# Output projection and expert routing of a mixture-of-experts layer: two stages, or one stage by batches

## The reference, cut to what matters

```python
hidden = resid + (ctx @ o_w + o_b)
xt = layer_norm(hidden, ln2_w, ln2_b).reshape(T, D)
logits = xt @ router_w
probs = softmax(logits)
top1 = argmax(probs)
top2 = argmax(where(m1 > 0, -inf, logits))
loc1 = cumsum(m1, axis=0) - 1
loc2 = cumsum(m2, axis=0) - 1 + m1.sum(axis=0)
m1 = m1 * (loc1 < C)
m2 = m2 * (loc2 < C)
g1, g2 = (probs * m1).sum(-1), (probs * m2).sum(-1)
xin = einsum('tec,td->ecd', d1 + d2, xt)
```

## Time and profile before

| | us |
|---|---|
| median of 3 runs | 2369.15 (2369.07 to 2370.01) |
| profiled execution, its own time | 2373.17 |
| its span, first to last instruction | 2371.40 |
| DVE busy | 1503.7 (63% of the span) |
| POOL busy | 815.1 (34%) |
| PE busy | 1682.7 (71%) |
| ACT busy | 904.1 (38%) |

### The profile page before, as it was taken

The page is one execution under the profiler, slowest core; times in us unless marked ns, Lnnn a source line. Parts: engine busy times, 40 slices in busy tenths (PEclk is TensorE's granted clock), DMA queues, the critical chain, the costliest instruction groups (busy, mean ns, idle before and its releaser), DMA issues. The chain is left out here.

```text
span 2371.4 us, 37567 instructions
## 1 busy us (share of the span) xinstructions
PE 1682.7 (71%) x12976; PEld 1004.5 (42%) x12976; DVE 1503.7 (63%) x3125; ACT 904.1 (38%) x1669; POOL 815.1 (34%) x911
## 2 busy tenths in 40 slices
PE   4899999996207943599991076589999999610992
PEld 2333333335106732399991044333333333500772
DVE  7888888953502236677774584888889884450223
ACT  4377777773002310000000033437777776200330
POOL 3022222224473420278780670102222222445341
PEclk8599999996558976699996589669999999655996
DMA  4433443300014442000004000443333330001444
GB/s 124 108 73 93 100 111 61 64 2 0 22 49 127 137 127 73 0 1 0 0 0 44 18 10 36 139 78 64 57 62 62 56 56 2 0 29 54 134 137 126
DMA packets 124466, 144.60 MB, mean 61 GB/s; under 512 B 34336, under 2 KB 74656, under 8 KB 123296
## 3 DMA queue, kind: packets, MB, share of 16 engines
q1 hardware_dynamic: 105648, 121.14, 22.1%
q0 software_dynamic: 8192, 16.86, 2.1%
q10 hardware_dynamic: 10480, 4.73, 0.8%
HBM read 96.17 MB, written 45.71 MB: 60 GB/s over the span
## 5 line engine op out<-in xcount | busy, mean ns | idle before, releaser
L723 DVE TENSOR_REDUCE mx<-pA 128x1 f32<-128x512 f32 (+3 forms) x1216 | 723.5, 656 | 46.5 <-PE pA L588 25.1
L748 ACT ACTIVATE wt<-pB 128x512 f32<-128x512 f32 (+1 forms) x1216 | 606.2, 583 | 254.2 <-PE pB L631 254.1
L588 PE MATMUL pA<-ka,qa 48*128 48x512 bf16 (+3 forms) x1536 | 413.2, 344 | 30.9 <-PEq L285 16.6
L631 PE MATMUL pB<-qa,ka 51*128 51x512 bf16 (+3 forms) x1536 | 389.6, 334 | 32.4 <-ACT wt L748 27.5
L788 POOL TENSOR_SCALAR_AFFINE_SELECT wt<-wt 128x512 f32<-128x512 f32 x256 | 162.4, 634 | 676.5 <-ACT wt L748 676.5
L650 PE MATMUL pC<-wt,va 128*32 128x512 f32 (+3 forms) x3072 | 332.5, 506 | 1.3 <-POOL wt L788 1.3
L588 PEld LDWEIGHTS pA<-ka,qa 48*128 48x128 bf16 x1536 | 138.6, 95 | 252.7 <-DVE mx L723 179.4
L1176 POOL DMA_INDIRECT y<-eo,dest x128 | 122.5, 957 | 185.0 <-issue 112.5
L592 PE MATMUL pA<-future_lo,pick_lo 64*128 64x64 bf16 x1024 | 184.3, 196 | 0.0
L592 PE MATMUL pA<-future_hi,pick_hi 64*128 64x64 bf16 x1024 | 181.0, 191 | 0.0
L631 PEld LDWEIGHTS pB<-qa,ka 51*128 51x128 bf16 x1536 | 119.5, 94 | 127.6 <-ACT wt L748 114.9
(11 more groups left out here) (249 smaller groups left out, 2533.8 us busy)
## 6 DMA issues: line engine op xcount, KB each, us to landing
qa<-qk_parts SPq DMA_DIRECT2D x384, 64.0 KB
ka<-qk_parts SPq DMA_DIRECT2D x384, 64.0 KB
w<-in_L_ffn_fc_w_dram SPq DMA_DIRECT2D x64, 256.0 KB, 2.8
xi<-xin SPq DMA_DIRECT2D x32, 258.0 KB, 3.7
qk_parts<-qp SPq DMA_DIRECT2D x24, 256.0 KB, 2.6
qk_parts<-kp SPq DMA_DIRECT2D x24, 256.0 KB, 3.4
xin<-zero SPq DMA_DIRECT2D x4, 1032.0 KB, 9.6
qa<-mT SPq DMA_DIRECT2D x256, 3.0 KB
```

What stands on the lines that cost most here:

```text
L588: last = pe.matmul(out[:, k, :], qa[u % 3][0:KROWS, t * per + k, i * P:(i + 1) * P], ka[u % 3][0:KROWS, t * per + k, a:b], start=True, sto ...
L631: last = pe.matmul(pB[n % NB][:, k * (e - a):(k + 1) * (e - a)], ka[u % 3][rows, h, j * P:(j + 1) * P], qa[u % 3][rows, h, a:e], start=Tru ...
L723: vec.reduce_max(mx[a // HALF][:, i, t * per:(t + 1) * per], pA[n % NA][:, 0:per * (b - a)].rearrange("p (h k) -> p h k", h=per), AX).then ...
L748: act.activation(wt[g % NW][:, heads, 0:e - a], pB[n % NB][:, 0:per * (e - a)].rearrange("p (h q) -> p h q", h=per), ACT.Exp).then_inc(exp ...
```

## The change

`ffn_route` goes away as a block. Its instructions become part of `ffn_output`, batch by batch, so the routing's tiles have 8 x 16 = 128 columns, and there are four times as many instructions on them. `ffn_output` is written out without loops. The places go on from batch to batch: the sums of a batch are carried over into the first tile of the next. First choices of batch b - 1 are routed and their rows scattered after the moments of batch b; second choices are found and counted with them but sent after the last batch, and the gates follow at the end. Where the counts, the places or the kept choices have to live longer than a batch, they have their own memory; `kept` is now copied from the one-hot choice, and the place is made by adding the running sum and subtracting the tile's own. ACT's order interleaves the exponential of a batch with the square root of the next; PE's has the counts of batch b - 1 behind the projection of batch b + 1. POOL's has the scaling of later batches between the scatters of earlier ones.

The diff, cut to its core (in the new `ffn_output`; `two` is `range(2)`, `tiles[b]` and `col[b]` are the slices of batch b):

```diff
-    c["restart"] = core.sb(ctx, "restart", [P, E, TILES])
+    c["restart"] = core.sb(ctx, "restart", [P, E, BT])
...
+                def scatter(n, b):
+
+                    pool.wait_ge(xn_kept, 2 * b + 2)
+                    pool.wait_ge(send_ready, n * BATCH + b + 1)
+                    for t in range(b * BT, (b + 1) * BT):
+                        pool.indirect_dma_start(
+                            out=w["xin"], out_offset=bass.IndirectOffsetOnAxis(ap=keep["send"][:, n, t:t + 1], axis=0),
+                            in_=xt[:, t, :], in_offset=None).then_inc(sent, 16)
+
+                bias(0)
+                bias(1)
+                numbers(0)
+                scaled(0)
+                bias(2)
+                scaled(1)
+                bias(3)
+                pool.wait_ge(c["wiped"], 16 * WIPES)
+                for b in range(BATCH):
+                    scatter(0, b)
+                    if b + 2 < BATCH:
+                        scaled(b + 2)
+                pool.wait_ge(sent, 16 * TILES)
+                numbers(1)
+                for b in range(BATCH):
+                    scatter(1, b)
+                pool.wait_ge(sent, 16 * 2 * TILES)
...
-                staggered(pe, project, logits)
+                def counts(b):
+
+                    pe.wait_ge(one_ready, 2 * b + 2)
+                    for n in two:
+                        flat = one[n][:, :, :].rearrange("p t e -> p (t e)")
+                        pe.matmul(pCount[:, n, 0, :], c["upper"][:, :], flat, start=True, stop=True)
+                        last = pe.matmul(pCount[:, n, 1, :], c["ones"][:, :], flat, start=True, stop=True)
+                    last.then_inc(counted, 1)
+
+                project(0)
+                project(1)
+                logits(0)
+                for b in range(1, BATCH):
+                    if b + 1 < BATCH:
+                        project(b + 1)
+                    counts(b - 1)
+                    logits(b)
+                counts(BATCH - 1)
...
+                side_by_side(1)
+                root(0)
+                transposed(1)
+                logits(0)
+                for b in range(1, BATCH):
+                    if b + 1 < BATCH:
+                        side_by_side(b + 1)
+                    weights(b - 1)
+                    root(b)
+                    if b + 1 < BATCH:
+                        transposed(b + 1)
+                    logits(b)
+                weights(BATCH - 1)
...
+                def choices(b):
+
+                    p = prob[:, tiles[b], :]
+                    vec.wait_ge(exps_ready, b + 1)
+                    link(vec.reduce_sum(total[:, :], p, AX))
+                    link(vec.reciprocal(recip[:, :], total[:, :]))
+                    link(vec.tensor_tensor(p, p, over_e(recip[:, :]), ALU.mult))
+                    top(p, 0, b)
+                    link(vec.scalar_tensor_tensor(logit2[:, :, :], one[0][:, :, :], LOWEST, L[:, tiles[b], :],
+                                                  ALU.mult, ALU.add))
+                    top(logit2[:, :, :], 1, b)
+
+                def located(n, b):
+
+                    place_in = loc[n][:, tiles[b], :]
+                    link(vec.tensor_copy(tot[n][:, :, :], pCount[:, n, 1, :].rearrange("p (t e) -> p e t", e=E)))
+                    if b > 0:
+                        link(vec.tensor_tensor(tot[n][:, :, 0], tot[n][:, :, 0], run[n][b - 1][:, :, BT - 1], ALU.add))
+                    link(vec.tensor_tensor_scan(run[n][b][:, :, :].rearrange("p e t -> p (e t)"),
...
+                    link(vec.scalar_tensor_tensor(place_in, pCount[:, n, 0, :].rearrange("p (t e) -> p t e", e=E), -1.0,
+                                                  run[n][b][:, :, :].rearrange("p e t -> p t e"), ALU.add, ALU.add))
+                    link(vec.tensor_tensor(place_in, place_in, pCount[:, n, 1, :].rearrange("p (t e) -> p t e", e=E),
+                                           ALU.subtract))
+                    link(vec.tensor_copy(kept[n][:, tiles[b], :], one[n][:, :, :]))
+
+                def sends(n, b):
...
+                    vec.tensor_copy(keep["send"][:, n, tiles[b]], place[:, :]).then_inc(send_ready, 1)
+                    vec.wait_ge(send_ready, n * BATCH + b + 1)
+
+                moments(0)
+                normal(0)
+                for b in range(1, BATCH + 1):
+                    if b < BATCH:
+                        moments(b)
+                    largest(b - 1)
+                    choices(b - 1)
+                    if b < BATCH:
+                        normal(b)
+                    vec.wait_ge(counted, b)
+                    located(0, b - 1)
+                    sends(0, b - 1)
+                    located(1, b - 1)
+                for b in range(BATCH):
+                    sends(1, b)
...
-        ffn_route(core, keep, w, c, tag)
```

More of the change, by code:

```diff
@@ L803, in ffn_output @@
         sem = lambda n: core.sem(ctx, n + tag)
+        two = range(2)
         rows, cT = sb("ctx_rows", [P, BCOL]), sb("ctxT", [P, SEQ])
@@ L808, in ffn_output @@
         pT, pO, pX, pL = ps("pT_o", [P, SEQ]), ps("pO", [P, BCOL]), ps("pX_o", [P, SEQ]), ps("pL", [P, BT * E])
+        pCount = ps("pCount", [P, 2, 2, BT * E])
         (rows_ready, bias_added, cT_done, cT_ready, o_done, o_used, var_ready, std_ready, xn_ready, xn_kept, xT_done,
-         xT_ready, l_done, l_kept, dve, pool_chain) = (sem(n) for n in (
+         xT_ready, l_done, l_kept, dve) = (sem(n) for n in (
              "rows_ready", "bias_added", "octx_T_done", "octx_T_ready", "o_done", "o_used", "var_o", "std_rdy_o",
[L812 to L822, removed]
+             "xn_ready_o", "xn_kept", "oxn_T_done", "oxn_T_ready", "l_done", "l_kept", "dve_o"))
+        G, B = [P, TILES, E], [P, BT, E]
+        prob, kept, loc = sb("prob", G), [sb(f"kept{n}", G) for n in two], [sb(f"loc{n}", G) for n in two]
+        shifted, logit2, work, one = sb("shifted", B), sb("logit2", B), sb("work_r", B), [sb(f"top{n}", B) for n in two]
+        tot = [sb(f"tot{n}", [P, E, BT]) for n in two]
+        run = [[sb(f"run{n}_{b}", [P, E, BT]) for b in range(BATCH)] for n in two]
+        best, first, total, recip = (sb(n, [P, BT]) for n in ("best", "first", "total", "recip"))
+        gate, weighed, gates = sb("gate", [P, 2, TILES]), sb("weighed", G), sb("gate_sum", [P, TILES])
+        at, dropped, place = sb("at", [P, BT]), sb("dropped", [P, BT]), sb("place", [P, BT])
+        used, inside = sb("used", [P, E]), sb("inside", [P, E, CC])
+        max_found, exps_ready, one_ready, counted = (sem("max_found"), sem("exps_ready"), sem("one_ready"), sem("counted"))
+        send_ready, sent, number_set = sem("send_ready"), sem("sent"), sem("number_set")
+        over_e = lambda v: v.unsqueeze(2).to_broadcast([P, v.shape[1], E])
+        over_t = lambda v, nt=BT: v.unsqueeze(1).to_broadcast([P, nt, E])
+        col = [slice(b * BCOL, (b + 1) * BCOL) for b in range(BATCH)]
+        tiles = [slice(b * BT, (b + 1) * BT) for b in range(BATCH)]
+        L = keep["logits"][:, :].rearrange("p (t e) -> p t e", e=E)
         with nc.Block() as block:
@@ L897, in batch, with weights, moments @@
                     act.wait_ge(l_done, b + 1)
-                    act.copy(keep["logits"][:, bass.ds(b * BT * E, BT * E)], pL[:, :]).then_inc(l_kept, 1)
+                    act.copy(L[:, tiles[b], :], pL[:, :].rearrange("p (t e) -> p t e", e=E)).then_inc(l_kept, 1)
+                def weights(b):
+                    act.wait_ge(max_found, b + 1)
+                    act.activation(prob[:, tiles[b], :], shifted[:, :, :], ACT.Exp).then_inc(exps_ready, 1)
                 side_by_side(0)
                 transposed(0)
[L902 to L905, removed]
+                side_by_side(1)
[11 more added lines that the diff above has]
+                weights(BATCH - 1)
             @block.vector
             def _(vec):
[L909 to L913, removed]
+                link = Chain(vec, dve).link
+                def moments(b):
+                    hidden = keep["hid"][:, col[b]]
                     vec.wait_ge(bias_added, b + 1)
@@ L926, in batch @@
                     reached(vec, xT_done, b)
[L927 to L964, removed]
@@ L980, in _ @@
[L980 to L988 removed]
+                    vec.wait_ge(one_ready, 2 * b + n + 1)
```

122 lines of the change are left out of this document (45 added, 77 removed).

## The result

The changed kernel takes **2333.15 us** (median of 4 runs, 2331.61 to 2337.55) where the kernel before takes 2369.21 beside it: ratio 0.985, 95% interval 0.9833 to 0.9867, a gain of 36 us. It is faster, as forecast, and inside the range, but the gain is nearly twice the 19 us of the forecast. The profiled execution took 2332.93 us (span 2331.1).

What follows compares the result with a forecast made beforehand. POOL's 64 scatters bound the stage, so their start counts. 101.0 us to the last send plus 61.9 gives 162.9 a layer, winning 10.1 and 9, together 19: 2369.15 - 19 = 2350 us, range 2326 to 2364.

Steps and rivals of the forecast that it cites:

- The mechanism: Routing stage: scatters start per batch, at 42.8 us instead of 81.2; POOL idles between groups, DVE's rounds of some 22 us pace.
- the straight line: DVE routing instructions: price interpolated between 4 and 512 columns, giving 0.292 us at 128 columns.
- the blocks beside POOL's scaling: Routing rounds: DVE instructions with two SBUF operands wait for POOL's running instruction to end; 11.6 us a layer.
- The no-blocking rival: Routing beside POOL's scaling: DVE and POOL run side by side, the 11.6 us a layer fall away; 2327 us, chance 0.18.
- nothing more is given back: Denies the rival for routing: blocks at upper bound, casts waiting for scatters, dearer instructions; 2357 to 2366 us, chance 0.15.
- the instructions shrink: Denies the rival that DVE's 128-column routing instructions keep the 512-column price; 2451 us, chance 0.08.
- Two of the signs: Stage timeline: first scatter 40 to 46 us after the start, last group at about 102.
- the path to the last send: Routing stage, from its start to the last batch's send of first choices: 101.0 us.
- From the last send to the experts: End of the stage: first scatter, spacings at 1.41, second series and final 8.10 us; sum 61.9 us.
- The two rules weighed: Routing: table load taken as 1.28 us, not about 2.66; scatter spacing beside DVE as 1.41, not 1.26.
- The second rival: ACT's table loads: each change of function costs two loads, 7.7 us in all; 2358 us, chance 0.07.

Runs made afterwards that it cites:

- the control: The changed kernel run once more with no edit; 2332.48 us.
- second_late: Changed kernel without POOL's scaling, counts ahead of the next projection, second choices of all batches found after the last first send; 2295.36 us.

## Why the prediction was right, and where its size was off

**The mechanism** holds, but for one term: the prediction let instructions with one SBUF operand run free, and a copy of that kind was stopped too (last section). 3.2 of the 9.2 us stand at this copy; that the two-operand instruction behind it would have waited in its place is likely, but no run shows it. The first scatters start half a stage earlier, POOL idles between groups, and DVE's rounds are the pace, though they took 20.4, 20.7 and 14.4 us rather than some 22. The 128-column instructions cost 0.292 us as the straight line said, and the blocks beside POOL's scaling are there and cost what they last. The no-blocking rival gave 2327 us, nearer to the measured time than 2350, and is wrong all the same: the blocks were seen, lengthened and taken away, each time with the matching change. Of the other rivals: the Exp begins 0.01 us after its table load has ended, so a change of function costs one load of 1.28 us; the casts (L1060) average 188 ns, so nothing more is given back there; and the instructions shrink.

**The size.** The measured 2333 us lies below the forecast's own range of 2340 to 2358; it is inside the whole range only because that reaches down to the no-blocking case. Two of the signs came early as well: the first scatter at 39.9 us, where 40 to 46 were named, and the last group at 95.4 instead of about 102. In the first layer the stage was forecast at 162.9 us and took 155.0. The step that failed is the path to the last send, 101.0 forecast and 94.6 measured:
- The blocks, 11.6 forecast, were 9.2. In batch 1 DVE arrived 1.4 us into POOL's first scaling instruction, so less of it was left to wait for; in batches 1 and 2 a scan got through between the two, and those that read PSUM ran on beside them.
- TensorE's parts came sooner. The logits of batch 0 were kept 20.2 us into the stage instead of 21.8; the eight transposes took 1.09 us, where those of before took 1.97 at a granted clock of 0.55 in the stretch from 541 to 551 us, nearly the lower of its two levels (1.2 of 2.4 GHz), against 0.73 now (rows below). The wait for the counts was 0.85 us instead of 1.6. The two middle rounds, blocks aside, were 0.6 to 0.8 us shorter each. Together 3.6 to 4 us, and not all of it the change's: in the control the same transposes took 1.38 us at 0.66, and the fourth group came 1.0 us later.
- From the last send to the experts 60.3 us instead of 61.9: the spacing of the last group beside DVE was 1.27 us, not 1.41.

The first 10 us of the stage in the kernel before, then in the changed one (busy time by stretch, columns as above; the clock is the third number from the end):

```profile
541.00:551.00 10.00, 6.64 (x31) 6.00 (x32) 0.67 (x3) 4.47 (x5) 4.65 (x2) 0.55 0.00 0
541.00:551.00 10.00, 6.41 (x34) 5.94 (x35) 1.32 (x3) 4.70 (x5) 4.80 (x3) 0.73 0.00 0
```

The second layer was credited with 9 us, of which 1.2 were for a quicker TensorE that was to stay; its stage came out as long as the first's and won 15.7. The two stages together won 33.7 us in these traces, 31.7 in the control's, against 19. That leaves 2 to 4 us of the measured 36 outside the stages, within the 9 us by which that part differs from trace to trace; I take it for no effect of the change.

**The two rules weighed.** The table load: the trace after decides for the row, 1.28 us, against the 2.66 us with a drain that the Trainium skill (ScalarE: Activation LUTs, What ACT_TABLE_LOAD costs) gives; no drain shows between load and Exp. (The second rival put that time down to a second load, the page puts it down to the drain; the rows show neither.) The spacing: beside 128-column products the scatters of the four groups came at 1.27 to 1.29 us, against 1.26 without, so for these the Trainium skill (SBUF — State Buffer, Who interferes with whom) was nearer than my 1.41, which was taken beside 512-column work and does stand there.

**Open.** Which DVE instructions lengthen a scatter, and why not all of 512 columns do (below), wasn't tried.

## What to carry to other kernels

Cutting a serial stage into batches wins the overlap and pays for what the new order puts ahead of the sends; hold both in two numbers (here 31 won, 14 to 16 paid a layer) before adding them up, and ask what the price is made of. Here it was the second choices and the blocks, and with both out of the rounds the last group of scatters started 7.4 us ahead of the first scatter of the kernel before. Then look at what the new overlap puts beside each other: an elementwise pass on GpSimd that was free beside one-operand work stopped VectorE's two-operand chain for 9 us a layer, and folding it into an instruction that was there anyway won nearly half as much again as the change. Keep in the paced round only what the next consumer needs; here the second choices could wait.

## What the runs showed of the hardware that was not expected

- A copy with one SBUF operand, 128 columns, SBUF to SBUF, is stopped too: 0.226 us alone, 1.28 beside POOL's scaling. I had taken only two-operand instructions to be. The copy of the same size out of PSUM ran at 0.29 us beside it. The Trainium skill (SBUF — State Buffer, Who interferes with whom) says that copies can enter a mode that takes the port shared with GpSimd; the rows agree.
- Between two POOL instructions one that was stopped gets through, and the next with all its inputs in SBUF is stopped again: in batch 0 scan, copy and product end at 575.41, 577.47 and 579.84, and POOL's three instructions at 575.13, 577.38 and 579.69. It goes the other way too: POOL's second scaling instruction, 2.17 us in batch 0, took 2.39 and 2.40 in batches 1 and 2, where the scan of 0.42 us began within 0.01 us of it (597.61 and 597.61, 618.35 and 618.34).
- Scatters are not lengthened by every DVE instruction beside them. In second_late 512-column products of 0.69 us left them at 0.96 us, and one that met the 512-column scan and the addition behind it took 1.33; in the kernel before the first ones took 1.17 beside products of the same size. Beside the 128-column work of the changed kernel their mean was 0.98 us, without DVE beside them 0.96.
